# A selective-scan kernel: two of 24 units a chunk weighed by VectorE in PSUM, and the fp32r remainder made by TensorE

## The reference, cut to what matters

```python
x_dbl = jnp.einsum('bkdl,kcd->bkcl', xs, x_proj_w)      # 4 directions k, 192 channels d, 4096 positions l
dts = x_dbl[:, :, :6]; Bs = x_dbl[:, :, 6:22]; Cs = x_dbl[:, :, 22:]
delta = softplus(einsum('bkrl,kdr->bkdl', dts, dt_proj_w) + dt_proj_b)
def step(h, inp):                                       # over the 4096 positions
    ul, dl, Bl, Cl = inp
    h = exp(dl[..., None] * A) * h + (dl * ul)[..., None] * Bl[:, :, None, :]
    return h, einsum('bkdn,bkn->bkd', h, Cl)            # 16 states n
```

## Time and profile before

| | us |
|---|---|
| median of three timed runs (lowest, highest) | 11102.96 (11083.56, 11105.95) |
| the profiled execution, its own time | 11114.08 |
| its span, first to last instruction | 11112.4 |
| mean granted clock of TensorE, share of full | 0.954 |

### The profile page before, as it was taken

One profiled execution on the slowest core, in us unless ns is written; L12 is line 12 of the kernel. 1 busy time (PEld: TensorE's weight loads), 2 busy tenths in 40 slices (PEclk: granted clock), 3 DMA queues, 4 the chain that ended last, 5 costly groups with the idle time before them and its releaser, 6 DMA issues. The chain is left out here.

```text
span 11112.4 us, 345302 instructions
## 1 busy us (share of the span) xinstructions
PE 9796.2 (88%) x142892; PEld 6546.6 (59%) x142892; DVE 9404.3 (85%) x5727; ACT 8689.8 (78%) x15618; POOL 9035.1 (81%) x3978
## 2 busy tenths in 40 slices
PE   8978888888888888888888888888888889799999
PEld 5645555555555555555555555555555555588888
DVE  7869999998999999989999998999999999555554
ACT  3468888888888888888888888888888888345453
POOL 1169999999999999999999999999999999534330
PEclk9989999999999999999999999999999999899999
DMA  3356666666666666666666666666666666322220
GB/s 103 108 153 160 167 174 171 161 167 170 174 161 167 177 167 162 168 173 167 159 167 175 166 161 166 175 170 162 172 177 164 159 171 163 84 75 64 70 70 13
DMA packets 547249, 1647.95 MB, mean 148 GB/s; under 512 B 148562, under 2 KB 149362, under 8 KB 542872
## 3 DMA queue, kind: packets, MB, share of 16 engines
q1 hardware_dynamic: 484248, 1416.10, 50.0%
q10 hardware_dynamic: 61440, 209.76, 6.1%
HBM read 1251.98 MB, written 373.29 MB: 146 GB/s over the span
## 5 line engine op out<-in xcount | busy, mean ns | idle before, releaser
L1004 POOL TENSOR_TENSOR HC<-H,crep 128x1024 f32<-128x1024 f32 x3072 | 7203.9, 2383 | 358.0 <-PE psum L714 277.7
L779 DVE TENSOR_TENSOR_SCAN H<-E,car,psum 128x1024 f32<-128x1024 f32 x2304 | 5271.4, 2333 | 344.8 <-PE psum L691 111.2
L880 ACT ACTIVATE E<-dlr,am 128x1024 f32<-128x1024 f32 x3072 | 3497.2, 1145 | 917.2 <-DVE H L779 868.6
L714 PE MATMUL psum<-HC,sely 128*32 128x512 f32 x12288 | 2307.0, 635 | 83.4 <-POOL HC L1004 65.2
L779 DVE TENSOR_TENSOR_SCAN H<-E,psum 128x1024 f32<-128x1024 f32 x768 | 1713.5, 2273 | 173.4 <-PE psum L691 78.1
L691 PE MATMUL psum<-diagp,dluT 128*32 128x128 f32 x49152 | 1630.3, 276 | 256.0 <-DVE H L779 240.8
L691 PE MATMUL psum<-diag,dluT 128*32 128x128 f32 x49152 | 1692.7, 280 | 145.7 <-issue 121.1
L691 PEld LDWEIGHTS psum<-diagp,dluT 128*32 128x32 f32 x49152 | 1387.0, 111 | 681.0 <-DVE H L779 488.9
L691 PEld LDWEIGHTS psum<-diag,dluT 128*32 128x32 f32 x49152 | 1448.2, 112 | 496.0 <-issue 377.3
L862 ACT ACTIVATE sdl<-dluT,blt 128x192 f32<-128x192 f32 x4096 | 1507.5, 444 | 0.0
L680 PE MATMUL psum<-idn,sdl 128*128 128x128 f32 x6144 | 953.2, 305 | 566.2 <-DVE H L779 566.2
(11 more groups left out here) (143 smaller groups left out, 10428.2 us busy)
## 6 DMA issues: line engine op xcount, KB each, us to landing
dlr<-scr_dl SPq DMA_DIRECT2D x3072, 128.0 KB, 4.2
dur<-scr_dlu SPq DMA_DIRECT2D x3072, 128.0 KB, 3.3
crep<-scr_bc SPq DMA_DIRECT2D x512, 256.0 KB, 6.4
crep<-scr_bc SPq DMA_DIRECT2D x1024, 128.0 KB, 3.0
scr_dlu<-dlu SPq DMA_DIRECT2D x256, 384.0 KB, 3.1
scr_yk<-yt ACTq DMA_DIRECT2D x256, 384.0 KB, 3.0
scr_dl<-dlt ACTq DMA_DIRECT2D x128, 384.0 KB, 4.4
scr_dl<-yt ACTq DMA_DIRECT2D x128, 384.0 KB, 4.2
```

The source lines that it names most:

```text
L714: r = e.matmul(yps[32 * j:32 * j + 32, cols], sely[:], HC[:, (3 * i + j) % NHC, cols], start=g == 0 and k != 0 and not second(m), stop=g = ...
L779: e.tensor_tensor_scan(H[:, un % NH, ::step], decay[:, ::step], drive[:, ::step], init, ALU.mult, ALU.add).then_inc(scan_done)
L880: e.activation(E[:, un % NE, :], dlr[:, slot(m, j), :], ACT.Exp, scale=am[:, ae:ae + 1]).then_inc(exp_done)
L1004: e.tensor_tensor(HC[:, un % NHC, :], H[:, un % NH, :], crep[:, g, :], ALU.mult).then_inc(hc_done)
```

## The change

Four things are changed in the scan phase, and a constant `less` is added (minus one on the diagonal from row 64 on, else zero; 102 x 102).

1. **Two units are VectorE's own** (`OWN`): units 20 and 21 of each chunk (turns 8 and 9 of the odd step, group 1). Their scan writes onto its own drive in PSUM, VectorE weighs them itself straight behind, and GpSimd skips them. ScalarE takes their last column from PSUM, one unit at a time. Their piece of PSUM is released by the weighing and, where there is a carry, by that copy.
2. **The remainder is made by TensorE**: at turn 6, after `fill(8)` and the half of `sum_y` of that turn, it projects once more into the same piece (`rest`, rows 0 to 101) and subtracts `sx` with an fp32r product. ScalarE casts rows 64 to 101 into `sx` at its turn 7 (`keep_rest`), and with that the piece of `x` is released. VectorE's `split` is gone.
3. **The side jobs move**: `dt` from turns 6 and 8 to 8 and 9 (ScalarE's softplus from 8 and 10 to 9 and 11), the stores of `dl` one turn later each, GpSimd's `dlu` of the even step from turn 8 to 10.
4. **GpSimd's `diagp`** goes from turns 7 and 9 to turns 8 and 9 of the odd step.

```diff
-    POOL_AT = (7, 9)
+    OWN = tuple(n % 2 == 1 and x in (8, 9) for n in range(2) for x in range(12))
+    POOL_AT = (8, 9)
...
     def side_jobs(n, x):
             if x == 4 and c < NCHUNK:
                 jobs += [("x", c)]
             if x == 6 and c < NCHUNK:
+                jobs += [("rest", c)]
+            if x == 8 and c < NCHUNK:
                 jobs += [("dt", 2 * c)]
-            if x == 8 and c < NCHUNK:
+            if x == 9 and c < NCHUNK:
                 jobs += [("dt", 2 * c + 1)]
...
-        ring += side_jobs(*divmod(un, 12))
+        ring += [job for job in side_jobs(*divmod(un, 12)) if job[0] != "rest"]
...
     def bank_free(e, *job):
         i = place_of[job] - NP
-        if i >= 0:
-            e.wait_ge(released[ring[i][0]], ring[i][1] + 1)
+        if i < 0:
+            return
+        name, n = ring[i]
+        if name == "unit" and own(n):
+            e.wait_ge(own_hc_done, owns(n + 1))
+            if has_carry(n):
+                e.wait_ge(own_carried, own_carries(n))
+        else:
+            e.wait_ge(released[name], n + 1)
...
     def tensor(e):
+        def rest(c):
+            k = steps[2 * c][1]
+            e.wait_ge(sx_copied, c + 1)
+            for sub in range(2):
+                x = input_of(c, sub)
+                for h in range(2):
+                    e.matmul(output_of(c, sub, C + NR), wx[:, k, h, 0:C + NR], x[:, h], start=h == 0, stop=False)
+                r = e.matmul(bank("x", c)[0:C + NR, sub * 512:(sub + 1) * 512], less[:], sx[:, c % 2, sub * 512:(sub + 1) * 512],
+                             start=False, stop=True)
+            r.then_inc(rest_left)
...
     def vector(e):
-        def split(c):
-            e.wait_ge(sx_copied, c + 1)
-            e.tensor_tensor(sx[64:C + NR, c % 2, :], bank("x", c)[64:C + NR, :], sx[64:C + NR, c % 2, :], ALU.subtract).then_inc(sx_split)
...
+            out, at = H[:, others(un) % NH, :], others(un) - NH
+            if own(un):
+                out = drive
+            elif at >= 0:
+                e.wait_ge(hc_done, at + 1)
...
+        def weigh(un):
+            b, k, ci, half, m, g, j = place(un)
+            e.wait_ge(scan_done, un + 1)
+            e.wait_ge(crep_in[load_of(g)], 64 * (m // 2 + 1))
+            if un >= NHC:
+                e.wait_ge(y_summed, (un - NHC) // 3 + 1)
+            e.tensor_tensor(HC[:, un % NHC, :], bank("unit", un), crep[:, g, :], ALU.mult).then_inc(own_hc_done)
...
             scan(un)
-            if c < NCHUNK and n % 2 == 0 and x == 6:
-                split(c)
+            if own(un):
+                weigh(un)
...
     def scalar(e):
+        def keep_rest(c):
+            e.wait_ge(rest_left, c + 1)
+            e.copy(sx[64:C + NR, c % 2, :], bank("x", c)[64:C + NR, :]).then_inc(sx_split)
...
+        def own_carry(un):
+            last = TC - 1 if place(un)[1] < 2 else 0
+            e.wait_ge(own_hc_done, owns(un + 1))
+            e.copy(car[:, cell(un):cell(un) + 1], bank("unit", un)[:, last:last + 1]).then_inc(own_carried)
...
                 if x == 5 and c < NCHUNK:
                     project(c)
-                if x == 8 and c < NCHUNK:
+                if x == 7 and c < NCHUNK:
+                    keep_rest(c)
+                if x == 9 and c < NCHUNK:
                     delta(2 * c)
-                if x == 10 and c < NCHUNK:
+                if x == 11 and c < NCHUNK:
                     delta(2 * c + 1)
-                if x == 11 and c < NCHUNK:
                     turn_b(c)
...
     def pool(e):
-            if un:
+            if un and not own(un - 1):
                 weigh(un - 1)
-                if x == 8 and n + 2 < NSTEP:
+                if x == 10 and n + 2 < NSTEP:
                     delta(n + 2)
```

More of the change, by code:

```diff
@@ L333, in scan_phase @@
     selb = T("selb", [C, 128], F32R)
+    less = T("less", [C + NR, C + NR], F32R)
     selt = T("selt", [C, NDIAG], F32R)
@@ L441, in last_of, with own, owns, others @@
                    and kind(un) in want.get("kinds", (DIRECT, DIAGONAL, SCALED)))
+    def own(un):
+        return OWN[un % 24]
+    def owns(un):
+        return un // 24 * sum(OWN) + sum(OWN[:un % 24])
+    def others(un):
+        return un - owns(un)
+    in_H = [un for un in range(NUNIT) if not own(un)]
+    def ends(t, a, b):
+        return t[:, a:b + 1:b - a] if b > a else t[:, a:b - 1 if b else None:b - a]
     def slot(m, j):
@@ L467, in has_carry, with own_carries @@
         return 0 <= un < NUNIT and place(un)[2] < NCH - 1
+    pairs_to = list(itertools.accumulate(int(has_carry(un) and not own(un)) for un in range(0, NUNIT, 2)))
+    own_to = list(itertools.accumulate(int(has_carry(un) and own(un)) for un in range(NUNIT)))
     def carries(un):
-        m, x = divmod(un, 12)
-        line, rest = divmod(m, 2 * NCH)
-        return 6 * (line * (2 * NCH - 2) + min(rest, 2 * NCH - 2)) + (x // 2 + 1 if rest < 2 * NCH - 2 else 0)
+        return pairs_to[un // 2]
+    def own_carries(un):
+        return own_to[un]
     def second(m):
@@ L564, in in_crep @@
             if c:
-                e.wait_ge(hc_done, max(last_of(2 * c - 1, g=g) for g in groups) + 1)
+                last = max(last_of(2 * c - 1, g=g) for g in groups)
+                e.wait_ge(hc_done, others(last + 1))
+                e.wait_ge(own_hc_done, owns(last + 1))
             g0, n = groups[0], len(groups)
@@ L619, in tensor, with input_of, output_of, project @@
     def tensor(e):
-        def project(c, sub):
+        def input_of(c, sub):
             b, k, ci, _ = steps[2 * c]
             t0 = t_of(k, ci) + sub * 512
+            if k % 2:
+                return u[:, :, :].rearrange("p a (h w) -> p a h w", w=HW)[:, :, :, t0 // HW:(t0 + 512) // HW]
+            return u[:, :, t0:t0 + 512]
+        def output_of(c, sub, rows):
+            o = bank("x", c)[0:rows, sub * 512:(sub + 1) * 512]
+            return o.rearrange("p (w h) -> p h w", h=HW) if steps[2 * c][1] % 2 else o
+        def project(c, sub):
+            k = steps[2 * c][1]
             if sub == 0:
@@ L711, in sum_y @@
             if sub == 0:
[L712 removed]
+                e.wait_ge(hc_done, others(3 * (i + 1)))
+                if owns(3 * (i + 1)) > owns(3 * i):
+                    e.wait_ge(own_hc_done, owns(3 * (i + 1)))
             for j in range(NJ):
@@ L725, in side_job @@
                 project(n, 1)
+            elif name == "rest":
+                rest(n)
             elif name == "dt":
@@ L733, in tensor @@
         side_job("x", 0)
+        side_job("rest", 0)
         side_job("dt", 0)
@@ L771, in scan @@
             e.wait_ge(exp_done, un + 1)
[L772 to L776, removed]
+            out, at = H[:, others(un) % NH, :], others(un) - NH
[3 more added lines that the diff above has]
+                e.wait_ge(hc_done, at + 1)
+                if has_carry(in_H[at]):
+                    e.wait_ge(carried, carries(in_H[at]))
+            if ci and own(un):
+                e.wait_ge(own_carried, own_carries(un - 24))
+            elif ci:
                 e.wait_ge(carried, carries(un - 24))
             step = 1 if k < 2 else -1
-            e.tensor_tensor_scan(H[:, un % NH, ::step], decay[:, ::step], drive[:, ::step], init,
+            e.tensor_tensor_scan(out[:, ::step], decay[:, ::step], drive[:, ::step], init,
                                  ALU.mult, ALU.add).then_inc(scan_done)
+        def weigh(un):
[5 more added lines that the diff above has]
+            e.tensor_tensor(HC[:, un % NHC, :], bank("unit", un), crep[:, g, :], ALU.mult).then_inc(own_hc_done)
         e.wait_ge(consts_in, NCONST)
@@ L784, in vector @@
         e.tensor_copy(selb[:], selbf).then_inc(ve_set)
+        e.tensor_copy(less[:], lessf).then_inc(ve_set)
         e.tensor_copy(dtw[:], dtwf).then_inc(dtw_made)
@@ L924, in scalar @@
         project(0)
+        keep_rest(0)
         out_bc(0)
@@ L945, in scalar @@
                     out_bc(c)
-                if x == 9:
+                if x == 10:
                     out_dl(2 * c)
-                if x == 11:
-                    out_dl(2 * c + 1)
+            if n < NSTEP and n % 2 and c < NCHUNK and x == 0:
+                out_dl(2 * c + 1)
             if x == 6 and n:
                 store_y(n - 1)
-            if un % 2 == 0 and has_carry(un - 1):
+            if has_carry(un - 1) and own(un - 1):
+                own_carry(un - 1)
+            elif un % 2 == 0 and has_carry(un - 1):
                 carry(un - 1)
@@ L1782, in constants @@
     dtm[C:, 0] = 1
+    less = np.zeros((C + NR, C + NR), f)
+    less[64:, 64:] = -np.eye(C + NR - 64)
     sely = np.zeros((128, 32), f)
```

31 lines of the change are left out of this document (14 added, 17 removed).

## The result

The changed kernel takes 11,970.98 us, the median of four runs (11,963.18 to 11,974.24); the kernel before took 11,104.45 beside it. The ratio is 1.0781, with a 95% interval of 1.0762 to 1.08: slower by 7.8%. The forecast was 11,770 and its range went to 12,080.

The account below looks back on a forecast made before the run. VectorE's order sets the pace, with GpSimd also near full. Work 63.8, stalls 4.4 + 3.4 + 2.0 and small waits 0.3 make 73.9 us a chunk against 68.7: 11,770 us; own range 11,500 to 11,980, 8 in 10 within 11,390 to 12,080.

Parts of the forecast that it names:

- B: Units 13 and 14: the fill of 13 waits for ScalarE's second softplus; 3.4 us a chunk (1.0 to 4.5).
- C: VectorE's weighing of unit 21 waits for TensorE's sum, which stands behind fill 22; 2.0 us a chunk (1.5 to 3.5).
- The work: VectorE's new work without stalls: 61.3 us plus 2.5 for two own weighings, 63.8 us a chunk.
- The scan into PSUM: VectorE's in-place scan: no surcharge, 2.33 us; upper bound 2.4 us a chunk more, as a rival 12,080, chance 0.05.
- the own weighing: VectorE weighing its own unit: 1.25 us with its start, at most 1.7, taken from the nearest row.
- Stall A: Unit 9: its fill needs the piece of `x`, free only after `keep_rest`; 4.4 us a chunk (3.1 to 5.5).
- The small waits: VectorE's remaining small waits for drives after the change: 0.3 us a chunk.
- The table switches: ScalarE's table loads take 1.28 us without a drain; rival with a drain: 4.1 us a chunk more, 12,290, chance 0.01.
- GpSimd's relief: Rival: 4.8 us less on GpSimd wins, the three stalls stay under 4.6 us; 10,740, chance 0.10.
- TensorE as the bound: Rival: TensorE, with 63.5 us of work, makes fills late throughout; 2.5 us a chunk more, 12,090, chance 0.10.

Follow-up runs that it names:

- run 4: The changed kernel without TensorE's second projection and subtraction (`rest`); ScalarE's second cast stays, so the remainder is wrong: 11,507.55 us, ratio 1.0363 to the kernel before.
- run 5: The changed kernel with ScalarE's second softplus one turn earlier, at turn 10: 11,790.95 us, ratio 1.0621 to the kernel before.
- run 3: The changed kernel with TensorE's half of the sum ahead of the fill in turns 20 and 21: 11,680.21 us, ratio 1.0517 to the kernel before.
- run 1: The kernel before plus VectorE's two own units and the new `diagp` turns; remainder by `split`, side jobs at their old turns: 11,508.76 us, ratio 1.0361.
- run 8: As run 1, but only unit 20 is VectorE's own and unit 21 goes back to GpSimd: 11,103.68 us, ratio 1.0003 to the kernel before.
- run 10: The kernel before with VectorE's `split` called after unit 7 in place of unit 6, nothing else: 10,866.93 us, ratio 0.9787.
- run 12: As run 10, with GpSimd's second part of `diagp` at turn 11 in place of 9: 10,824.58 us, ratio 0.9745 to the kernel before.

## Why the prediction was right, and what in it was not

The direction and the mechanism of the three stalls were right; the loss was 867 us where 666 were forecast (by the chunk 6.6 against 5.2), and the time lies at the upper end of the forecast's own range. That it isn't further off is in part luck: B was 0.8 us a chunk too large, C 1.6 too small. Step by step:

- **The work.** 63.8 us forecast, 63.7 measured. The scan into PSUM costs nothing extra, which I had only by bounds, and the own weighing takes 1.225: shown by the profile after.
- **Stall A, unit 9.** 4.4 forecast, 4.55 measured, and 4.3 of it go without `rest` (run 4). Shown. In the chunk shown `rest` takes 4.14 and not 3.8 us: its two fp32r products take 1.4 and not 0.7, its fp32 products 2.7 and not 3.1. The ring itself has 1.1 us of the wait.
- **Stall B, unit 13 and 14.** 3.4 forecast, 2.6 measured. Its cause is shown by run 5. The forecast was too large by a table load that ScalarE does before the `dt` product is there (1.4 us), and too small by the fill at the lower clock (1.0 us in the chunk shown).
- **Stall C, the weighing of unit 21.** 2.0 forecast, 3.6 measured, the largest error of the sum: 1.6 us a chunk, some 200 us. The mechanism is shown by run 3, and that it stands apart from `rest` by run 1. I had allowed 0.5 us for TensorE at 1.2 GHz; the fill and the sum at that level cost 1.2 on average, and the carry, fill 23 and the last half of the sum are 0.8 longer than their terms. The measured wait lies just outside the bounds that I gave C (1.5 to 3.5).
- **The small waits.** 0.3 forecast, 1.0 measured: unit 18's 0.6 us, which the kernel before has too, was not carried over. I had put the small waits before down to drives and taken GpSimd off the path after the change; this one is a wait for GpSimd in both.
- **The table switches.** The loads cost what their rows say: the exp before one ends at 4400.03 (4398.88 + 1.15), the load starts at 4400.05 and takes 1.28, and the softplus starts at 4401.34, 0.01 us after its end. The Trainium skill ("ScalarE: Activation LUTs", section "What ACT_TABLE_LOAD costs") adds a drain of about 1380 ns to every switch. The trace disagrees: there is no such gap on either side of the load.
- **The rivals.** GpSimd's relief is real but small: it takes away the 1.8 us at unit 1, and two own units cost 2.5 us of VectorE's time (run 1), one costs 1.25 (run 8). TensorE as the bound falls by runs 1 and 4. I had called GpSimd near full; run 10 shows that at 68.8 us a chunk it was not what bound the kernel, and in run 12, at 66.6, its lateness begins to move instead of going away.

## What to carry to other kernels

When a job is taken out of a ring of buffers or moved in it, write down for each job which other one it waits for three places ahead, and what now stands ahead of it in its engine's order: a stage that was cheap because its successor needed its result anyway becomes a stall when the successor is another. An engine at 95% busy is not the bound for that alone; here a wait of 1.8 us on the engine that sets the pace was worth more than 2.4 us off the busier one (run 10 against run 8). And of several things that an instruction waits for, check by their end times which came last, as the profile's own answer was another at unit 18. Before work is moved between engines, try the order: moving one call by one unit gained 2.1%, where the change lost 7.8%.

## What the runs showed of the hardware that was not expected

- VectorE's in-place scan in PSUM, 1024 columns: 2339 ns (median), as into SBUF (2336).
- An fp32r product of 102 x 102 by 512 columns, added to what two fp32 products left in the piece, took 0.79 us (0.63 to the next start), where the `dt` product of 102 x 96 by 512 took 0.71 for two (4397.47). The clock isn't the reason: the granted clock over `rest` in the chunk shown is 1.00. What is was not tested.
- TensorE is at 1.2 GHz in the same place of many chunks, after idle times of 1 to 3 us, and just where VectorE waits for it: in the 48 chunks with neither addition the median of fill 22 is 1.94 us (1.09 at the full clock), and half a sum takes 1.93 in place of 1.06 in the chunk shown. Of 127 chunks, 61 have fill 22 at this level. The idle time before it is 2.0 to 3.0 us in these and hardly other in the rest, so that idle time alone doesn't decide it.
